# T4 of the first pair in a place of its own, the first W tile in four parts, and new orders for T1, T2, the last h, r's first loads and the tail's banks

## The reference, cut to what matters

```python
h   = x @ W.T + bias + (x @ A[id].T) @ B[id].T          # per batch, 2048 -> 2048
q   = h @ Wq.T; router = (q @ Wr.T) @ (keys @ Wr.T).T / sqrt(48) + log_rel
top = top_k(router, 8)
w   = softmax(q . keys[top] / sqrt(64) + log_rel[top])
aux = (w @ values[top]) @ Wvd.T @ Wvu.T
u   = clip(0.5 * log1p(var(h)) / mean(log1p(var(h))) + 2.5 * sigmoid(gelu(h @ Wu1.T + bu1) @ Wu2.T + bu2), 0, 5)
gate = sigmoid(gate_w1 * clip((u - 0.5) / 1.5, 0, 1) + gate_bias), 0 where below 0.05
out = x + h + gate * aux
```

## Time and profile before

| | us |
|---|---|
| median of 3 runs | 1962.99 (1960.79 to 1964.92) |
| the profiled execution, its time on the device | 1958.85 |
| its span, first to last instruction | 1957.1 |
| PE busy within the span | 1924.3 (98%) |
| DVE busy | 1250.9 (64%) |
| ACT busy | 693.6 (35%) |
| POOL busy | 407.1 (21%) |
| DMA, 16 engines, mean rate over the span | 213 GB/s |

### The profile page before, as it was taken

The page is one execution under the profiler, slowest core; times in us unless marked ns, Lnnn a source line. Parts: engine busy times, 40 slices in busy tenths (PEclk is TensorE's granted clock), DMA queues, the critical chain, the costliest instruction groups (busy, mean ns, idle before and its releaser), DMA issues.

```text
span 1957.1 us, 24741 instructions
## 1 busy us (share of the span) xinstructions
PE 1924.3 (98%) x8618; PEld 1567.3 (80%) x8618; DVE 1250.9 (64%) x1639; ACT 693.6 (35%) x1059; POOL 407.1 (21%) x275
## 2 busy tenths in 40 slices
PE   8998999999999999999999999999999999999998
PEld 6776888888888888888888887778788888888886
DVE  5686587455468736546863644677566677676676
ACT  3332334333233433323333322345443233233332
POOL 2210132030023202002320200220343332332332
PEclk9998999999999999999999999999999999999999
DMA  8867677551367745146774424666888776777797
GB/s 289 287 241 243 219 243 231 160 178 58 133 207 234 230 150 170 65 148 211 231 226 143 164 90 169 227 219 213 284 270 273 249 237 226 242 236 234 239 359 285
DMA packets 196353, 416.56 MB, mean 213 GB/s; under 512 B 26820, under 2 KB 27844, under 8 KB 196102
## 3 DMA queue, kind: packets, MB, share of 16 engines
q1 hardware_dynamic: 150726, 325.83, 50.8%
q10 hardware_dynamic: 45504, 89.15, 12.0%
HBM read 317.37 MB, written 97.52 MB: 212 GB/s over the span
## 4 chain that ended last, share of the span: by engine, by line
PE 88%; issue 4%; DVE 3%; DMA 2%; ACT 1%; POOL 1%; SPq 1%; ACTq 0%; DVEq 0%; POOLq 0%
PE bank L1781 18%; PE bank L1782 18%; PE bank L1783 18%; PE bank L1817 6%; PE bank L1818 6%; PE bank L1819 6%; PE bank L1929 1%; PE bank L1931 1%; PE bank L1930 1%; PE bank L1709 1%; PE bank L1721 1%; PE bank L1722 1%; PE bank L1835 1%; PE bank L1834 1%; PE bank L1898 1%
## 5 line engine op out<-in xcount | busy, mean ns | idle before, releaser
L1781 PE MATMUL bank<-xop,wsp 128*128 128x512 f32 x1792 | 708.7, 395 | 19.7 <-DVE wsp L1257 10.7
L1782 PE MATMUL bank<-xop,wsp 128*128 128x512 f32 x1792 | 700.5, 391 | 0.0
L1783 PE MATMUL bank<-xop,wsp 128*128 128x512 f32 x1792 | 699.5, 390 | 0.0
L1781 PEld LDWEIGHTS bank<-xop,wsp 128*128 128x128 f32 x1792 | 337.5, 188 | 104.8 <-DVE xop L1257 11.1
L1782 PEld LDWEIGHTS bank<-xop,wsp 128*128 128x128 f32 x1792 | 337.7, 188 | 73.8 <-issue 3.8
L1783 PEld LDWEIGHTS bank<-xop,wsp 128*128 128x128 f32 x1792 | 337.3, 188 | 71.9
L868 ACT ACTIVATE wsp<-wraw 128x1024 fp32r<-128x1024 f32 x184 | 195.0, 1060 | 527.1 <-PE bank L1783 498.3
L1257 DVE TENSOR_TENSOR wsp<-wraw,wsp 128x1024 fp32r<-128x1024 f32 x184 | 232.2, 1262 | 192.7 <-ACT wsp L868 192.2
L850 POOL TENSOR_TENSOR r_h<-r_h,r_x 128x512 f32<-128x512 f32 x128 | 176.7, 1381 | 365.9 <-DMA r_h<-h_dram 325.2
L1817 PE MATMUL bank<-h_sp,wu 128*128 128x512 f32 x512 | 201.3, 393 | 2.1 <-DVE stage L1346 2.0
L1818 PE MATMUL bank<-h_sp,wu 128*128 128x512 f32 x512 | 200.4, 391 | 0.0
(11 more groups left out here) (172 smaller groups left out, 1950.7 us busy)
## 6 DMA issues: line engine op xcount, KB each, us to landing
xraw<-in_x SPq DMA_DIRECT2D x248, 256.0 KB, 4.1
wraw<-in_w SPq DMA_DIRECT2D x123, 512.0 KB, 3.8
wraw<-t_dram SPq DMA_DIRECT2D x88, 512.0 KB, 3.6
h_dram<-stage ACTq DMA_DIRECT2D x128, 256.0 KB, 2.7
hraw<-h_dram SPq DMA_DIRECT2D x128, 256.0 KB, 4.1
r_x<-in_x SPq DMA_DIRECT2D x128, 256.0 KB, 4.3
r_h<-h_dram SPq DMA_DIRECT2D x128, 256.0 KB, 3.5
out<-o_st ACTq DMA_DIRECT2D x96, 256.0 KB, 3.9
```

Of the source, the lines that this page charges most:

```text
L1781: pe.matmul(ps, wsp[:, slot, 0, f], x_hi(i), start=(k == 0), stop=False)
L1782: pe.matmul(ps, wsp[:, slot, 0, f], x_lo(i), start=False, stop=False)
L1783: last = pe.matmul(ps, wsp[:, slot, 1, f], x_hi(i), start=False, stop=(k == HT - 1))
```

## The change

- T4 no longer passes through the ring `wraw`. It has its own place, `t4_raw`, which is the half of `sums` that M4 is the first to write; its load (`load_t4`) stands in SP's turn after the x tiles and waits until the T4 before it is stored; DVE makes it last in its turn, every second turn from 14 to 28; the first `add_sums` into that half waits for the eighth store.
- T1 is made in turns 2, 4, 6, 8 to 12 (before: 1 to 6, 9, 11), T2 in 13 to 20 (before: 8, 10, 12 to 17). ACT stores T1 after x is split, not before.
- W tile 0 is loaded and split in four parts of 128 KB (256 columns, two blocks k each), interleaved with the x tiles; PE waits for each part. The 16 low-rank matmuls of tile 0 stand behind its 24 others. The low-rank weights are loaded after x tile 7.
- `o_st` and `r_h` change places, and the first `load_r` waits for tile 222 and the h stores up to M5 only (the stores of all h are waited for at the 17th).
- `finish` of tile 223 comes ahead of `add_sums` of tile 222 on DVE.
- The steps of batch 7's query (copy, sum, hi, lo) go to the ends of steps 20 and 22.
- In the tail batch 6's tiles 6 and 7 go to `u_ps[0]` and `u_ps[1]`, and batch 7's tiles go over all eight banks instead of four, with waits to match.

The core of the diff:

```diff
+        t4_raw = sums[:, 0, :, :].rearrange("p a s -> p (a s)")
...
-        r_h = at(at_wsp + 8 * K, "r_h", [P, 4, S])
-        o_st = at(at_wsp + 16 * K, "o_st", [P, 4, S])
+        o_st = at(at_wsp + 8 * K, "o_st", [P, 4, S])
+        r_h = at(at_wsp + 16 * K, "r_h", [P, 4, S])
...
-        T1_AT = dict(zip((1, 2, 3, 4, 5, 6, 9, 11), range(HT)))
-        T2_AT = dict(zip((8, 10, 12, 13, 14, 15, 16, 17), range(HT)))
-        T4_AT = {16 + o: o for o in range(HT)}
+        T1_AT = dict(zip((2, 4, 6, 8, 9, 10, 11, 12), range(HT)))
+        T2_AT = {13 + o: o for o in range(HT)}
+        T4_AT = {14 + 2 * o: o for o in range(HT)}
...
-        entries = [(g, 1, "t1", o) for g, o in T1_AT.items()] + [(g, 1, "t2", o) for g, o in T2_AT.items()] \
-            + [(g, 1, "t4", o) for g, o in T4_AT.items()]
+        entries = [(g, 1, "t1", o) for g, o in T1_AT.items()] + [(g, 1, "t2", o) for g, o in T2_AT.items()]
...
-            return kind == "t4" or kind == "tile" and g < PAIR and tile_of(g)[1] == M7
+            return kind == "tile" and g < PAIR and tile_of(g)[1] == M7
...
+            if b == NB - 2 and o in (6, 7):
+                return u_ps[o - 6]
...
-            return (q_ps, aux_bank, u_ps[2], u_ps[3])[o % 4]
+            return (s_ps, wz_ps, aux_bank, u_ps[3], u_ps[0], u_ps[1], u_ps[2], q_ps)[o % 8]
...
                         elif p == 0:
-                            wait_stored(sp, "t4", o)
+                            sp.wait_ge(t4_out, 16 * (o + 1))
...
+            def load_t4(o):
+                wait(sp, t4_out, 16 * o)
+                sp.dma_start(t4_raw, w[o, :, WT:2 * WT]).then_inc(t4_in, 16)
...
-                    stored(c // 2)
+                    stored(4 * HT * (c // 2 + 1))
...
                 if n == 0:
-                    sp.wait_ge(main_done, TILES)
-                    sp.wait_ge(wl_ready, TILES)
-                    stored(NPAIR - 1)
+                    sp.wait_ge(main_done, TILES - 1)
+                    stored(h_index(NPAIR - 1, M5, HT - 1) + 1)
+                if n == KT:
+                    stored(4 * HT * NPAIR)
                 wait(sp, r_ready, n - 3)
...
+            load_first(0)
             load_x11(0)
-            load_t(0)
             load_x11(1)
+            load_first(1)
             load_x11(2)
+            load_x11(3)
+            load_first(2)
+            load_x11(4)
+            load_first(3)
+            for k in range(5, HT):
+                load_x11(k)
             sp.wait_ge(ids_in, 16)
             load_a(0)
-            for k in range(3, HT):
-                load_x11(k)
             load_t(1)
             sp.dma_start(bias_sb[:], base_bias).then_inc(small_in, 16)
...
+                if g + 1 in T4_AT:
+                    load_t4(T4_AT[g + 1])
...
-                act.dma_start(t_dram[T4, o], w_raw("t4", o)).then_inc(t_out[W_PLACE["t4", o] % NWR], 16)
+                act.dma_start(t_dram[T4, o], t4_raw).then_inc(t4_out, 16)
...
+            def first_w_hi(j):
+                f = slice(j * WT // 4, (j + 1) * WT // 4)
+                if j < 3:
+                    act.wait_ge(t3_moved[j], 16)
+                    to_hi(wsp[:, 0, 0, f], t_res[:, 0, f]).then_inc(first_hi, 1)
+                else:
+                    act.wait_ge(t_moved[0], 16)
+                    to_hi(wsp[:, 0, 0, f], t_res[:, 0, f]).then_inc(wh_ready, 1)
...
             split_x_hi(0, M1, 0)
-            split_w_hi(0)
+            first_w_hi(0)
             split_x_hi(0, M1, 1)
             split_x_hi(0, M1, 2)
+            first_w_hi(1)
+            split_x_hi(0, M1, 3)
+            split_x_hi(0, M1, 4)
+            first_w_hi(2)
+            split_x_hi(0, M1, 5)
+            first_w_hi(3)
+            split_x_hi(0, M1, 6)
+            split_x_hi(0, M1, 7)
             act.wait_ge(consts, 3)
             split_a_hi(0)
-            for k in range(3, HT):
-                split_x_hi(0, M1, k)
             split_w_hi(1)
...
-                if g - 1 in T1_AT:
-                    store_t1(T1_AT[g - 1])
                 if g - 1 in T4_AT:
                     store_t4(T4_AT[g - 1])
...
+                if g - 1 in T1_AT:
+                    store_t1(T1_AT[g - 1])
...
-                    if k == 4 and c == 1:
-                        query_copy(EARLY)
-                    if k == 5 and c == 1:
-                        query_hi(EARLY)
...
+                    if k == 4 and c == 1:
+                        query_copy(EARLY)
+                    if k == 6 and c == 1:
+                        query_hi(EARLY)
...
-                wait_w(dve, "t4", o)
+                dve.wait_ge(t4_in, 16 * (o + 1))
                 dve.wait_ge(t_ready, t_count("t2", o))
-                dve.tensor_tensor(w_raw("t4", o), w_raw("t4", o), t_res[:, o, :], SUB).then_inc(t_ready, 1)
+                dve.tensor_tensor(t4_raw, t4_raw, t_res[:, o, :], SUB).then_inc(t_ready, 1)
...
+                    if seg == 0:
+                        dve.wait_ge(t4_out, 16 * HT)
...
-                if g in T4_AT:
-                    make_t4(T4_AT[g])
...
+                if g in T4_AT:
+                    make_t4(T4_AT[g])
+            finish(TILES - 1)
             add_sums(TILES - 2)
-            finish(TILES - 1)
             split_wu_lo(7)
...
-                    if k == 4 and c == 1:
-                        query_sum(EARLY)
-                    if k == 5 and c == 1:
-                        query_lo(EARLY)
...
+                    if k == 4 and c == 1:
+                        query_sum(EARLY)
+                    if k == 6 and c == 1:
+                        query_lo(EARLY)
...
-                    if k == 0:
+                    if g == 0 and k % 2 == 0 and k < 6:
+                        pe.wait_ge(first_lo, k // 2 + 1)
+                    if k == (6 if g == 0 else 0):
                         pe.wait_ge(wl_ready, g + 1)
...
-                    if o == 0 and q in (M1, M2, M7, M4):
+                    if o == 0 and g > 0 and q in (M1, M2, M7, M4):
...
+                if g == 0:
+                    for k in range(HT):
+                        lora_a_step(0, M1, k)
...
+                elif b == NB - 2 and o in (6, 7):
+                    pe.wait_ge(wtl_ready, (NB - 1) * TT + o - 3)
+                elif b == NB - 2 and o == 8:
+                    pe.wait_ge(last6_ready, 5)
...
-                elif o < 2:
-                    pe.wait_ge(last6_ready, BY_DVE - (o == 1))
-                elif o < 4:
-                    pe.wait_ge(ev_ready, KT - BY_DVE - (o == 3))
-                else:
-                    pe.wait_ge(last7_ready, o - 3)
+                elif o in (2, 4, 5, 7):
+                    pe.wait_ge(last6_ready, {2: 6, 4: 7, 5: 8, 7: 9}[o])
+                elif o in (3, 6):
+                    pe.wait_ge(ev_ready, {3: 6, 6: 7}[o])
+                elif o >= 8:
+                    pe.wait_ge(last7_ready, o - 7)
```

More of the change, by code:

```diff
@@ L232, in bass_adaln_ffn @@
         t_ready = sem("t_ready")
-        t_out = [sem(f"t_out{i}") for i in range(NWR)]
+        t3_moved = [sem(f"t3_moved{i}") for i in range(NWR)]
         v_in = [sem(f"v_in{i}") for i in range(HT)]
@@ L386, in is_stored @@
             kind, g = entries[n][2:4]
-            return kind == "t4" or kind == "tile" and g < PAIR and tile_of(g)[1] == M7
+            return kind == "tile" and g < PAIR and tile_of(g)[1] == M7
         def wait_stored(eng, kind, g):
             n = W_PLACE[kind, g]
-            eng.wait_ge(t_out[n % NWR], 16 * sum(is_stored(i) for i in range(n % NWR, n + 1, NWR)))
+            eng.wait_ge(t3_moved[n % NWR], 16 + 16 * sum(is_stored(i) for i in range(n % NWR, n + 1, NWR)))
         def wait_all_stored(eng):
+            eng.wait_ge(t4_out, 16 * HT)
             for place in range(NWR):
-                eng.wait_ge(t_out[place], 16 * sum(is_stored(i) for i in range(place, len(entries), NWR)))
+                eng.wait_ge(t3_moved[place], 16 + 16 * sum(is_stored(i) for i in range(place, len(entries), NWR)))
         def t_count(what, o):
             order = [(g, 0, "t1", i) for g, i in T1_AT.items()] + [(g, 1, "t2", i) for g, i in T2_AT.items()] \
-                + [(g, 2, "t4", i) for g, i in T4_AT.items()] + [(g, 3, "t3", i) for g, i in T3_AT.items()]
+                + [(g, 2, "t3", i) for g, i in T3_AT.items()] + [(g, 3, "t4", i) for g, i in T4_AT.items()]
             return [e[2:4] for e in sorted(order)].index((what, o)) + 1
@@ L541, in load_w @@
                         sp.wait_ge(t_ready, t_count(old, og))
-                    elif old == "t4":
-                        wait_stored(sp, "t4", og)
                     elif old == "wu":
@@ L560, in load_w @@
                     sp.dma_start(into, w[HT + g, :, WT:2 * WT]).then_inc(done, 16)
-                elif kind == "t4":
-                    sp.dma_start(into, w[g, :, WT:2 * WT]).then_inc(done, 16)
                 else:
@@ L1402, in h_lo, with first_w_lo @@
                 lo(h_sp[m % 4][:, 1, :], hraw[:, m % 4, :], h_sp[m % 4][:, 0, :]).then_inc(hl_ready, 1)
```

(20 more changed lines are left out.)

15 lines of the change are left out of this document (12 added, 3 removed).

## The result

| | before | after |
|---|---|---|
| median of the runs | 1962.88 us (1960.79 to 1964.92, 4 runs) | 1933.55 us (1932.99 to 1936.17, 4 runs) |
| ratio | | 0.9856, 95% interval 0.9842 to 0.9871 |
| profiled execution | 1958.85, span 1957.1 | 1933.54, span 1931.6 |
| mean granted clock, profiled execution | 0.996 | 0.999 |

The medians are 29.3 us apart, the two spans 25.5. The forecast was 1939 with 24.1 us for the spans, within 1933 to 1949.

What follows compares the result with a forecast made beforehand. PE is busy 1924.3 of 1957.1 us, so only what moves matmul starts counts. Terms 11.7 + 3.3 + 2.3 + 5.6 + 0.6 + 0.6 = 24.1 off 1958.85 give 1934.7, plus 4.1 to the median: 1939, range 1933 to 1949.

Steps and rivals of the forecast that it cites:

- T4 out of the ring: Tiles 20 and 24: their PE waits and the slow clock behind go, 11.7 us, bounds 9 to 11.8.
- T1 and T2 late: Tiles 7, 8 and 16: PE's waits on DVE behind late loads go, 3.3 us.
- I take 0: Turns 9 to 13: extra DMA traffic, 2.4 us too many, fits the two tiles of reserve; bounds -0.1 and 5.
- the first rival: DMA full in turns 9 to 13: rate falls to 330 GB/s, PE stands some 5 us, 1944; chance 0.15.
- The start: First W tile in parts: PE's first matmul at 6.0 instead of 7.72, gain 2.3 us, bounds 1.5 to 3.9.
- Between the parts: Passage to the second part: `finish` first 2.2, slow clock 1.6, r's earlier loads 1.8; 5.6 us, bounds 3.7 to 6.3.
- The query of batch 7: Batch 7's query behind `normalise`: takes 0.67 out of the way of a 0.7 wait; 0.6 us, 0 to 0.8.
- The tail: Last output tiles over eight banks: both PE bank waits go, but stores limit the gain to 0.6 us, 0 to 1.4.
- only the dents before the hole are won: Tail stores: the first of 28 comes no sooner, so only small dents before the hole are gained, 0.6 us.
- From spans to medians: Whole kernel: profiled execution lies 4.1 us below the median of the runs, so 1934.7 becomes 1938.9, taken as 1939.
- The second and third: T4's new place as tight as the ring, 1947.5, chance 0.10; slower, SP standing in `load_t4`, 1972, chance 0.03.

Runs made afterwards that it cites:

- the square of four runs: Changed kernel 1933.55 us; T1 and T2 in old turns 1939.46; T1, T2 and T4 all as before 1952.7; only T4 as before, through the ring, 1961.26.
- the fourth corner: Changed kernel with T4 back through the ring in turns 16 to 23, T1 and T2 left late: 1961.26 us, ratio 1.0006.

## Why the prediction was right, point by point

*T4 out of the ring, forecast 11.7.* Right in kind and in size. From after tile 16 to after tile 24 the trace gives 12.1: the waits of tiles 20 and 24 and the slow stretch are gone. SP's wait at `load_t4` cost nothing, as said. The working had treated the place apart from T1 and T2, though; the square of four runs says 13.2 with them early and 27.7 with them late. It also priced the place and the two turns for each T4 as one; the two turns are 17.1 of the 27.7.

*T1 and T2 late, forecast 3.3.* The step that failed in part is "the load is issued when tile 14 is split or the T1 before is made and has a turn to land", with "I take 0" for the DMA engines. The waits of tiles 7 and 8 went (3.0 in the lead), but that of tile 16, counted as gone, was 2.2 in place of 0.77, so the trace shows 1.5. The rate did not fall, as the first rival had it; it rose from 366 to 400 GB/s. The first T2's load took 6.9 us to land, more than a turn of 5.8, and came 1.8 us after DVE had asked; how much of that reached PE (0 to 3.8) hung on how early the ring had let it go. The figure of about 358 GB/s that the Trainium skill (DMA: Bandwidth & Descriptors, Where 436 GB/s comes from) gives for a core's traffic with HBM is passed by both rows, and the rows decide. My own cap for the stretch was the 366 of the earlier trace rows, and it was no cap either. The term's lower bound in the sum, 2, also doesn't follow from its working, which allows a cost of 5 against a gain of 3.3; and the 5.5 and 2.8 us late of the first rival count 29.3 us of tiles where the term has 29, by which they are 5.8 and 3.1.

*The start, forecast 2.3.* Trace 2.1 at tile 1, undoing it 2.6. The first matmul came at 6.04, forecast 6.0. The 0.23 pace began 5.3 us behind it, where before it was 7.27. Over the twelve profiled executions with the new start it began 3.0 to 6.1 us behind the first matmul, at 9.3 to 12.2 us, after 7 to 14 matmuls; so neither the distance nor the moment is fixed. That agrees with what the prediction cites from the Trainium skill (TensorE: Matmul & The Clock Gate, What's actually happening), a period that runs free of the kernel's start. But the start of tile 1 moved by 0.9 us only, since a PE that is fast early waits for x, for W or for the low-rank weights (0.66 at 14.92). That cover made the term narrower than its bounds.

*Between the parts, forecast 5.6.* Trace 6.0. The first load of r was issued at 1352.50, 1368.2 in the time of before; PE waited 0.34 for the query where I had 0.7. Undone one by one the two edits cost 3.1 (of which the trace places 1.4) and 5.0, where their shares were 3.8 with the slow clock and 1.8. The working had put the slow clock down to the wait for `finish`; with that wait gone and the query's back, the slow stretch came behind the query's.

*The query of batch 7, forecast 0.6.* Trace 0.8 between the matmuls around it; no run undoes it alone.

*The tail, forecast 0.6.* Too low; 1.8 to 2.0 between the traces of before and after, 1.3 to 1.7 by undoing it, against 1.4 at most by my bounds. The step that failed is "only the dents before the hole are won": the hole near the end went too, and PE's bank waits set the distance between the last stores and their sums.

*From spans to medians.* I carried the 4.1 us between the profiled execution of before and the median of its runs over to the changed kernel, which gave 1939 for 1934.7. That was the largest error: its first profiled execution and its median are the same, 1933.54 and 1933.55. A part of the distance is the clock. The runs of before have mean granted clocks of 0.994 to 0.997 and their times follow them: of 17 side by side, the four at 0.997 took 1955.1 to 1957.5 us, the six at 0.994 took 1962.1 to 1965.3. All nine runs of the changed kernel have 0.999 or 1.000, so most of the slow stretches behind waits are gone. But a part is chance: those nine still spread from 1931.5 to 1937.6 us, and when the kernel was run again its profiled execution was the fastest of five, 2.6 under their median. The medians were 29.3 us apart the first time and 26.5 (1960.63 and 1934.12) with 17 and 5 runs. So that the lower end of the range was met, and not its middle, is in part the draw.

*The rivals.* None came. The first had the right place (DMA in turns 9 to 13) and the wrong size: it cost 0 to 3.8 us at tile 16, from one execution to the next, plus a slow stretch behind the longest, and not 5. The second and third did not show; the run with T4 in each turn shows a case in which the third is real.

## What to carry to other kernels

Moves that draw on one store of slack don't add up: the same two-line shift of T1 and T2 gave 5.9 us beside T4's new plan and cost 8.6 without it. So price them together, by the places and queues they share, and part a plan that is two things (a place, a spacing) into its halves. A short wait costs more than its length where the clock may drop behind it, and the part that it adds varies between executions; so look at the granted clock of all runs before you carry the distance between one trace and the median over to another kernel. When a load comes late, look first at when it could be issued: here its time to land was much the same in executions with no wait and with the longest. And a rate seen in a full window need not be the most that can be had: the share was 0.99 at 366 GB/s, and 400 were moved in the next kernel, at 7.5 us to land in place of 6.0.

## What the runs showed of the hardware

The half pace comes behind some waits of PE and not behind others of the same length. In the traces of before, of the changed kernel and of the runs, the waits of 3.27, 3.36, 3.78, 4.58, 5.13, 6.98 and 10.93 us were all followed by 5 or more matmuls at 0.43 us. Of the shorter ones in the steady part, those of 2.0, 2.06 (twice), 2.11, 2.30 and 2.80 were, and those of 1.96, 1.97, 2.20, 2.22, 2.5, 2.52 and 2.79 were not. A window after the 2.52 us wait in the run with T4 in each turn, and one after the 10.93 of the fourth corner:

```profile
171.30:174.00 2.70, 2.70 (x13) 1.96 (x13) 1.55 (x3) 0.32 (x1) 0.00 (x0) 1.00 0.85 203
...
180.50:183.00 2.50, 2.50 (x7) 1.77 (x6) 2.50 (x4) 0.00 (x0) 0.00 (x0) 0.50 0.94 374
```

What tells the shorter waits apart is open. At the start the pace of 0.43 is not in the granted clock's rows: 12 matmuls took 4.69 us where the row says 1.00,

```profile
6.63:11.32 4.69, 4.69 (x12) 3.46 (x11) 3.14 (x6) 3.61 (x8) 0.00 (x0) 1.00 0.96 339
```

so there the distance between matmuls shows the pace, and the row does not.

A DVE pass over 4 KB rows has no fixed time. In the 14 traces (before, after and the twelve runs) 3178 two-operand passes of 128x1024 f32 ran beside no instruction of POOL, and every one took 1.20 to 1.23 us. Of the 2116 that POOL overlapped, by the profile's rough spans of POOL, about 600 took over 1.3 us and up to 2.36. The first T4 of the changed kernel is one (1.65 us), and so is the split behind it (2.31). In the run with the old tail, which had the longest wait at tile 16, four of the passes between the first T2 and the split of x22s took 2.28 to 2.32 us. What POOL did beside them was its sums of x. So these seem to cost DVE time just where its lead over PE is thin; no run takes them away.
